# Recurrence of a small hybrid network: the two waits ahead of the i gate's activation written in the other order

## The reference

```python
xi = xt @ U_i + b_i
xg = xt @ U_c + b_c
xo = xt @ U_o + b_o
def step(carry, xs):
    h, c = carry
    xi_t, xf_t, xg_t, xo_t = xs
    i_t = jax.nn.sigmoid(xi_t + h @ V_i)
    g_t = jnp.tanh(xg_t + h @ V_c)
    o_t = jax.nn.sigmoid(xo_t + h @ V_o)
    c_new = h * c + i_t * g_t
    h_new = o_t * jnp.tanh(c_new)
    return ((h_new, c_new), h_new)
```

## Time and profile before

| what | value |
|---|---|
| median of 3 runs | 447.81 us (445.8 to 448.85) |
| the profiled execution's own time | 448.33 us |
| its span, first to last instruction | 446.5 us |
| share of the span busy: PE, PEld, DVE, ACT, POOL | 65%, 50%, 59%, 47%, 5% |
| first to last start of L368, 256 steps | 123.21 to 441.37 us |
| mean step | (441.37 - 123.21) / 255 = 1.248 us |
| granted TensorE clock, 160 to 300 us | 0.50 of full speed, its level of 1.2 GHz |

### The profile page before, as it was taken

One profiled execution on the slowest core, in us unless ns is written; L12 is line 12 of the kernel. 1 busy time (PEld: TensorE's weight loads), 2 busy tenths in 40 slices (PEclk: granted clock), 3 DMA queues, 4 the chain that ended last, 5 costly groups with the idle time before them and its releaser, 6 DMA issues.

```text
span 446.5 us, 11853 instructions
## 1 busy us (share of the span) xinstructions
PE 290.3 (65%) x3273; PEld 222.9 (50%) x3273; DVE 261.2 (59%) x2309; ACT 210.9 (47%) x1169; POOL 21.0 (5%) x38
## 2 busy tenths in 40 slices
PE   1899889989855555555555555555555555555553
PEld 1466447643545555544555555544555555445552
DVE  0976454655356666666666666666666666666664
ACT  1488352253544444444444444444444444444442
POOL 6920000000000000000000000000000000000000
PEclk9999999799975555555555555555555555555555
DMA  8400000000000000000000000000000000000000
GB/s 305 188 3 0 1 0 2 0 1 0 0 3 2 0 0 0 0 0 0 0 0 0 0 0 0 0 0 0 0 0 0 0 0 0 0 0 0 0 0 12
DMA packets 2828, 5.78 MB, mean 13 GB/s; under 512 B 1408, under 2 KB 1792, under 8 KB 2816
## 3 DMA queue, kind: packets, MB, share of 16 engines
q1 hardware_dynamic: 2384, 4.55, 2.7%
q10 hardware_dynamic: 432, 1.08, 0.6%
HBM read 5.50 MB, written 0.13 MB: 13 GB/s over the span
## 4 chain that ended last, share of the span: by engine, by line
ACT 36%; PE 35%; DVE 14%; issue 11%; DMA 1%; ACTq 1%; SPq 0%; DVEq 0%
PE bank L659 18%; ACT bank L380 16%; ACT go L374 11%; ACT gi L368 6%; DVE ha L933 6%; DVE terms_a L933 4%; PE bank L439 2%; PE bank L419 2%; PE bank L391 2%; PE bank L428 2%; DMA cst<-in_const 1%; PE bank L591 1%; PE bank L552 1%; PE bank L603 1%; ACTq L367 1%
## 5 line engine op out<-in xcount | busy, mean ns | idle before, releaser
L659 PE MATMUL bank<-ha,vparts 128*128 128x1 f16 x1536 | 95.5, 169 | 133.3 <-DVE ha L933 133.3
L659 PEld LDWEIGHTS bank<-ha,vparts 128*128 128x128 f16 x1536 | 74.7, 106 | 156.1 <-DVE ha L933 156.1
L368 ACT ACTIVATE gi<-bank 128x1 f32<-128x1 f32 x256 | 43.8, 171 | 167.4 <-PE bank L659 167.4
L930 DVE TENSOR_SCALAR go<-go 128x1 f32<-128x1 f32 x256 | 39.3, 153 | 86.5 <-ACT go L374 86.5
L380 ACT ACTIVATE bank<-bank,hc,gi 128x2 f32<-128x2 f32 x256 | 83.2, 325 | 0.0
L659 PE MATMUL bank<-hb,vparts 128*128 128x1 f16 x768 | 69.5, 165 | 0.0
L933 DVE CUSTOM_DVE_ANT_0 terms_a<-bank,go 128x3 f32<-128x3 f32 x256 | 41.1, 161 | 30.4 <-ACT bank L380 2.1
L655 PE MATMUL bank<-x,w5s 128*128 (+1 forms) x198 | 55.7, 357 | 0.2 <-DVE x L769 0.2
L468 PE MATMUL bank<-ones,w5s 128*128 128x8 f32 x198 | 55.4, 354 | 0.0
L939 DVE SCALAR_TENSOR_TENSOR cell<-bank,gi,hc 128x1 f32<-128x1 f32 x256 | 54.9, 214 | 0.0
L659 PEld LDWEIGHTS bank<-hb,vparts 128*128 128x128 f16 x768 | 53.9, 104 | 0.0
(11 more groups left out here) (215 smaller groups left out, 303.0 us busy)
## 6 DMA issues: line engine op xcount, KB each, us to landing
w3s<-in_w SPq DMA_DIRECT2D x1, 804.0 KB, 11.1
ltr<-in_later SPq DMA_DIRECT2D x1, 709.0 KB, 9.4
bias<-in_positions ACTq DMA_DIRECT2D x1, 704.0 KB, 6.9
bias<-in_positions SPq DMA_DIRECT2D x1, 704.0 KB, 8.1
w2s<-in_w SPq DMA_DIRECT2D x1, 640.0 KB, 10.4
w5s<-in_w SPq DMA_DIRECT2D x1, 576.0 KB, 11.8
w0s<-in_w ACTq DMA_DIRECT2D x1, 336.0 KB, 3.9
w1s<-in_w SPq DMA_DIRECT2D x1, 256.0 KB, 9.4
```

The source lines that it names most:

```text
L368: act.activation(gi[:], bank[pre + 1][:, at:at + 1], ACT.Sigmoid, scale=1.0 / PRE)
L659: return mm(bank[3 * parity + k][:, at:at + 1], vparts[:, part, k], h, start=False, stop=False, skip_group_check=True)
L930: ts(go[:, two, 3:4], o, -1.0, None, ALU.mult).then_inc(on("minus_o"), 1)
```

## The change

Lines 366 and 367 change places: the wait for `i_pre` is written first, the one for `cell_ready` second. Nothing else differs; TensorE's and VectorE's instructions are the same.

```diff
                 for u in range(STEPS_IN_BODY):
                     t, pre, at, two = base + u, (u // CHUNK) * 3, u % CHUNK, u % 2
+                    act.wait_ge(on("i_pre"), t + 1)
                     act.wait_ge(on("cell_ready"), t + 1)
-                    act.wait_ge(on("i_pre"), t + 1)
                     act.activation(gi[:], bank[pre + 1][:, at:at + 1], ACT.Sigmoid, scale=1.0 / PRE)
```

## The result

The changed kernel takes 430.92 us (median of 4 runs, 428.89 to 432.61) against 447.4 us for the kernel before (4 runs). The ratio is 0.9647, with a 95% interval of 0.961 to 0.9685: 3.5% faster. The forecast was 432.4 us, with a range of 427.0 to 437.5.

A forecast was written before the change was run, and what follows sets the result against it. The prediction took a chain of hand-overs between ScalarE, TensorE and VectorE as the bound. A gain of 0.06 us in each of 256 steps, other terms 0, gave 15.4 us less: median 432.4 us, 3.4% faster, range 427 to 437.5.

The forecast's parts named there:

- What bounds the kernel: Whole recurrence: a chain of hand-overs between ScalarE, TensorE and VectorE; time taken off each step counts 256 times.
- First term: Way from i_pre to L368: falls from 0.08 to 0.02 us, a gain of 0.06 us a step.
- rival B: Smaller gain, by step 0's longer period at L380: 0.045 us a step, 436.3 us; chance 0.10.
- Second term: L370 and L374 behind L368: distances of 0.07 and 0.05 us stay, gain 0, at best 0.02 a step.
- Rival A: Deeper gain: L368 to L370 falls to 0.05 us; 0.07 or 0.08 a step, 429.9 or 427.3 us; chance 0.22.
- rival D: Slower: waiting L368 holds back L370, overlap lost, L370 0.19 us behind; costs 0.06 a step, 463.2 us; chance 0.05.
- Third term: Separate wait for cell_ready ahead of L368: covered with 0.07 us to spare, cost 0.
- Fourth: Other limits of a shorter step: TensorE's idle time and clock (0.50, 1.2 GHz), VectorE's L930; cost 0 each.
- Rival C: No gain: L368 still starts 0.08 us behind the matmul, through TensorE's semaphore or idle start; 447.8 us; chance 0.08.

The follow-up runs named there:

- gi_two: Changed kernel with gi in two columns used in turn; L368 waits only for i_pre, cell_ready's separate wait moves ahead of L370; 432.09 us, 0.9676 of before.
- gates_separate: Changed kernel with L380's two waits swapped as well, so hc_ready rides and gates goes into the separate wait; 446.03 us, 1.0018 of before.

## Why the prediction was right

- What bounds the kernel: right. Only the hand-over into L368 changed, and 255 steps carried it to the end.
- First term, 0.06 us a step: right. From i_pre to the start of L368 it is 83 ns before and 23 after, and most ordinary steps went from 1.247 to 1.187. By the mean it is a shade large, 1.245 - 1.187 = 0.058, since a few steps before were 7 ns shorter; over the recurrence 14.9 us where 15.4 was forecast. Reading it at L368 itself was better than reading it at step 0: rival B's 0.045 was the price of another form of the separate wait (below). The reversed swap at L380 cost 0.06 as well.
- Second term, 0: right. L370 and L374 kept their distances, and g_pre and o_pre did not become the bound. Rival A fell. The prediction cited the Trainium skill, "Perfetto Trace Analysis", "Per-engine timelines" (DVE / Act Engine Instruction), for L370 standing ready behind the waiting L368. The traces do not bear that rule out for this sequencer. In gi_two the separate wait ahead of L370 had its semaphore 144 ns before the i gate's activation had its own, and ran only 6 ns after that activation had started, in all 256 steps; in the changed kernel the register instruction behind L380 ran 5 ns after L380's start, although it waits for nothing. So the sequencer stood still behind an activation that waited with its riding wait, as rival D had it, but the overlap was not lost by that: L370 is still 0.07 behind. The estimate by the Trainium skill's "ScalarE: Activation LUTs", "What ACT_TABLE_LOAD costs", that L370 would follow only after 0.078 us, is not borne out by any run here: L368 takes 171 ns and L370 starts 68 behind it, an overlap of 103 ns and not of 93.
- Third term, the cover of cell_ready, 0.07 us: right. A delay of 0.062 cost nothing, one of 0.123 cost 0.037 a step. By the semaphores' own times (medians in the changed kernel) cell_ready is raised 0.146 us ahead of i_pre and has to be 0.06 ahead, the 0.083 of a separate wait less the 0.023 of the riding one. So the margin was 0.086, by which the longer delay should cost 0.123 - 0.086 = 0.037, as it did; I had left out that the riding wait takes its 0.02 in any case.
- Fourth, TensorE's clock: 0.50 in the middle of the recurrence after the change too, as in the earlier trace rows.
- Rival C fell with the chain after: the 0.08 were not TensorE's semaphore on its way. Rival D fell: L370 still overlaps L368. Rival B's price does not show in any ordinary step.
- Of the measured 16.5 us, 14.9 are the recurrence of the profiled executions; the rest is within the interval, 0.961 to 0.9685, which is 14.1 to 17.4 us.

## What to carry to other kernels

Where an activation has two waits and only one can ride on it, let the one that ends last ride, and put the early one in the separate wait, where it costs nothing as long as it comes some 0.06 us ahead. In this chain of short dependent steps that was worth 0.06 us each time; with the late one guessed wrong it costs as much. All of this was measured on ScalarE; no run here shows what a separate wait costs on another engine. Which is late is read from the trace, and it has to be read again after any edit that moves either producer; a loop body that holds the other order in one of its steps shows the price before the change is made.

## What the runs showed that I had not expected

An activation here never holds more than one wait, but the separate wait ahead of it can hold two, and then it has a price of its own, in which the order inside it counts. From the moment gates is raised to the start of L380: 24 ns when it rides; 84 when it is alone in the separate wait (gates_separate, ordinary steps); 73 when the wait holds hc_ready, then gates (step 0 of before and of the changed kernel); 106 when it holds gates, then hc_ready (step 0 of gates_separate, which is why that step took 1.27 and not 1.23). The instruction's own time shows where the difference comes from: where hc_ready is listed first, it has started before gates comes and ends 27 ns after it; where gates is listed first, it starts only 21 ns after gates and takes 38, against 17 with one semaphore. In each case L380 starts 45 to 47 ns after its end. So step 0 of the kernel before was not quite the change in reverse: it showed 0.049 where a lone separate wait costs 0.060.
